# Gates and their tanh first, eight fixed expert tiles with the lists moved behind them, two shared down products in another bank, a ring of six

## What is computed

```python
x = x + tanh(g_xattn[0]) * L0_xattn(layernorm(x), ctx)   # one head, keys of 32 context tokens
x = x + tanh(g_ffn[0])   * L0_ffn(layernorm(x))          # expert choice: each of 8 experts picks 64 tokens, attends among them
x = x + tanh(g_xattn[1]) * L1_xattn(layernorm(x), ctx)   # 16 heads, mask over the context
x = x + tanh(g_ffn[1])   * L1_ffn(layernorm(x))          # mixture of experts

# L1_ffn: normed = layernorm with gamma and beta
probs = softmax(normed @ router_w.T); top_v, top_i = top_k(probs, 2); gates = softmax(top_v)
for e in range(8):                                       # swiglu: silu(gate) * up, then down; width 384
    out += comb[:, e] * swiglu(normed, gate_up_w[e], down_w[e])
out += swiglu(normed, shared_gate_up_w, shared_down_w)   # shared expert of width 128
```

## Time and profile before

| | us |
|---|---|
| median of 3 runs | 318.01 (316.6, 318.01, 321.76) |
| profiled execution | 318.32 |
| span of the profiled execution | 316.4 |
| PE, DVE, ACT, POOL busy | 273.7, 231.8, 207.7, 155.1 |

### The profile page before, as it was taken

The page is one execution under the profiler, slowest core; times in us unless marked ns, Lnnn a source line. Parts: engine busy times, 40 slices in busy tenths (PEclk is TensorE's granted clock), DMA queues, the critical chain, the costliest instruction groups (busy, mean ns, idle before and its releaser), DMA issues.

```text
span 316.4 us, 7622 instructions
## 1 busy us (share of the span) xinstructions
PE 273.7 (87%) x2454; PEld 207.2 (65%) x2454; DVE 231.8 (73%) x702; ACT 207.7 (66%) x481; POOL 155.1 (49%) x202
## 2 busy tenths in 40 slices
PE   8787996896999896999888763969899999999995
PEld 4463352455677554687666651348799999999995
DVE  4468178956987755788989967899577777777765
ACT  2765599986577678976864743534577777878530
POOL 2524289023632628625022778781027888888700
PEclk9899999999999999999999955589999999999999
DMA  7790002100349999980000111113212222201074
GB/s 210 228 362 39 1 2 85 48 3 0 134 151 190 182 189 182 190 130 0 2 1 11 35 36 43 51 51 84 57 52 79 71 77 70 68 32 37 8 233 135
DMA packets 34613, 28.13 MB, mean 89 GB/s; under 512 B 3072, under 2 KB 32389, under 8 KB 33936
## 3 DMA queue, kind: packets, MB, share of 16 engines
q1 hardware_dynamic: 32192, 23.77, 33.6%
q0 software_dynamic: 2240, 3.72, 3.6%
q10 hardware_dynamic: 144, 0.15, 0.2%
HBM read 14.15 MB, written 14.40 MB: 90 GB/s over the span
## 4 chain that ended last, share of the span: by engine, by line
PE 33%; DVE 22%; issue 14%; ACT 12%; POOL 12%; DMA 4%; SPq 1%; POOLq 0%; DVEq 0%; ACTq 0%
PE bank L1201 29%; POOL expert_rows L850 11%; ACT w_high L559 2%; ACT w_scaled L557 2%; DMA wr<-in 2%; DVE bn_raw L867 1%; DVE nm L998 1%; DVE region_k L1000 1%; DVE region_x L1160 1%; DMA region_q<-expert_rows 1%; ACT x_hat L547 1%; DVE x L899 1%; PE bank L1425 1%; DVE region_k L966 1%; ACT x_hat L671 1%
## 5 line engine op out<-in xcount | busy, mean ns | idle before, releaser
L1185 DVE TENSOR_TENSOR region_k<-region_x,region_k 128x768 f16<-128x768 f32 (+1 forms) x33 | 30.6, 927 | 21.6 <-ACT region_k L721 21.6
L1201 PE MATMUL bank<-w_scaled,w_high 128*128 128x256 f16 x252 | 42.4, 273 | 0.1
L1201 PE MATMUL bank<-w_high,region_k 128*128 (+1 forms) x380 | 37.6, 220 | 3.3 <-DVE x L1175 2.5
L850 POOL DMA_INDIRECT expert_rows<-region_k,slot_dest x22 | 27.1, 1232 | 26.4 <-DVE region_k L1172 19.1
L824 POOL DMA_INDIRECT dispatched_rows<-region_t,slot x28 | 29.0, 1036 | 16.1 <-issue 8.3
L721 ACT ACTIVATE region_k<-region_x 128x768 f16<-128x768 f32 (+1 forms) x33 | 26.8, 812 | 14.2 <-DVE region_x L1160 14.2
L1201 PE MATMUL bank<-w_scaled,w_low 128*128 128x256 f16 x126 | 34.3, 273 | 0.0
L1201 PE MATMUL bank<-w_low,region_k 128*128 (+1 forms) x190 | 33.8, 220 | 0.0
L1201 PEld LDWEIGHTS bank<-w_high,region_k 128*128 128x128 f16 x380 | 30.8, 98 | 4.5 <-issue 4.1
L1160 DVE SCALAR_TENSOR_TENSOR region_x<-bank,region_w 128x768 f32<-128x768 f32 (+1 forms) x33 | 30.4, 921 | 3.2 <-ACT region_w L726 2.1
L1201 PE MATMUL bank<-filler 128*128 128x512 f16 x94 | 27.9, 418 | 3.9 <-DVE region_k L909 2.4
(11 more groups left out here) (246 smaller groups left out, 755.5 us busy)
## 6 DMA issues: line engine op xcount, KB each, us to landing
dispatched_rows<-pad_rows SPq DMA_DIRECT2D x8, 1048.0 KB, 18.4
w_scaled<-in SPq DMA_DIRECT2D x5, 1024.0 KB, 7.8
w_scaled<-dispatched_rows SPq DMA_DIRECT2D x21, 131.0 KB, 2.2
region_q<-expert_rows SPq DMA_DIRECT2D x3, 512.0 KB, 5.1
x<-in SPq DMA_DIRECT2D x4, 256.0 KB, 3.9
region_w<-in SPq DMA_DIRECT2D x2, 512.0 KB, 7.0
out<-x SPq DMA_DIRECT2D x3, 256.0 KB, 2.8
w_scaled<-in SPq DMA_DIRECT2D x1, 704.0 KB, 4.0
```

The costliest lines, as they stand in the source:

```text
L850: pool.indirect_dma_start(ytok, bass.IndirectOffsetOnAxis(dst[:, n, h:h + 1].bitcast(U32), 0), yv[n % 4][:, h * D:(h + 1) * D], None, boun ...
L1185: dve.tensor_tensor(hsplit[:, v, k:2 * k], hid[:, v, 0:k], hsplit[:, v, 0:k], ALU.subtract).then_inc(hidden_low, 1)
L1201: return pe.matmul(o, l, r, start=start, stop=stop)
```

## The change

1. **Gates first.** The two gates are loaded at the head of ACT's queue, ahead of the constants `c32`, and the tanh stands right behind the load of the activation table. The values `v0` of the cross-attention are scaled by the first gate in the copy that takes them out of PSUM; the multiplication of `rz` on DVE is gone. `wr0` has a semaphore of its own.
2. **Eight fixed tiles.** Tile n < 8 is always the first 256 rows of expert n, at row n x 2048. SP, PE and `slot_dest` take numbers instead of loaded values for them. The other 13 (`LISTED`) come from lists half as long (`TTAB` 32 to 16). The list work leaves the shared steps 1 and 2 and stands in the steps 8, 9 and 10 (tiles 1, 2 and 3); `gates_of_all` moves from step 3 to 2. SP waits for the lists only at tile 8, PE only before tile 7.
3. **Bank 6.** The down products of shared steps 1 and 3 go to bank 6 instead of 7, and wait for the emptying of two steps before instead of one.
4. **Ring of six.** SP's loaded tiles have six places instead of four. `slot_dest` moves from two steps ahead to its tile's own step.

The core of the diff:

```diff
-ROUNDS = -(-TILES // 4)
-TTAB = 4 * ROUNDS + 8
+LISTED = TILES - E
+ROUNDS = -(-LISTED // 8)
+TTAB = 8 * ROUNDS
+RING = 6
+DOWN_IN_6 = (1, 3)
...
+        def down_bank(s):
+            return bank[6] if s in DOWN_IN_6 else bank[7]
...
-            eng.dma_start(graw[:, 0:2], gx_in...).then_inc(gates_loaded, 16)
-            eng.dma_start(graw[:, 2:4], gf_in...).then_inc(gates_loaded, 16)
-            eng.dma_start(wr0[:, 0:E], wr0_in).then_inc(gates_loaded, 16)
+            eng.dma_start(wr0[:, 0:E], wr0_in).then_inc(wr0_loaded, 16)
...
-            eng.wait_ge(tiles, 1)
-            rows = [eng.value_load(trow_i[0:1, n:n + 1], min_val=0, max_val=E * REG) for n in range(AHEAD)]
             eng.wait_ge(w_low_done, CHUNKS)
             eng.wait_ge(sent, 16 * 2 * NS)
             for n in range(TILES):
-                wait(eng, rows_turned, n - 3)
-                wait(eng, dest_ready, n - 3)
-                row = rows[n] if n < AHEAD else eng.value_load(trow_i[0:1, n:n + 1], min_val=0, max_val=E * REG)
+                wait(eng, rows_turned, n - RING + 1)
+                wait(eng, dest_ready, n - RING + 1)
+                if n == E:
+                    eng.wait_ge(tiles, 2)
+                row = n * REG if n < E else eng.value_load(trow_i[0:1, n - E:n - E + 1], min_val=0, max_val=E * REG)
...
         def _(act):
+            act.dma_start(graw[:, 0:2], gx_in...).then_inc(gates_loaded, 16)
+            act.dma_start(graw[:, 2:4], gf_in...).then_inc(gates_loaded, 16)
             act.dma_start(c32[:, :], c32_in).then_inc(c32_loaded, 16)
             nc.scalar.preload_act_table(ACT.Exp)
+            act.wait_ge(gates_loaded, 32)
+            act.activation(tg[:, :], graw[:, :], ACT.Tanh).then_inc(tanh_done, 1)
...
-                    if b == 0:
-                        act.wait_ge(gates_loaded, 48)
-                        act.activation(tg[:, :], graw[:, :], ACT.Tanh).then_inc(tanh_done, 1)
...
-            after_hidden = {0: top2_apart, 1: tiles_placed, 2: windows_packed, 3: gates_of_all}
+            after_hidden = {0: top2_apart, 2: gates_of_all, STEP_OF[1]: tiles_numbered, STEP_OF[2]: tiles_placed, STEP_OF[3]: windows_packed}
...
                 pe.wait_ge(hidden_low, s + 1)
-                wait(pe, rows_ready, s)
+                if s == DOWN_IN_6[0]:
+                    pe.wait_ge(tiles, 1)
+                wait(pe, rows_ready, s - 1 if s <= DOWN_IN_6[-1] + 1 else s)
...
                 if late:
-                    pe.wait_ge(tiles, 2)
-                    load_window(0)
-                    e = experts()
-                    load_window(1)
+                    pe.wait_ge(rows_ready, DOWN_IN_6[-1] + 1)
                     turn(0)
                     down(s - 1, None)
```

More of the change, by code:

```diff
@@ L429, in build @@
         padded = sem("padded")
-        rows_loaded = [sem(f"rows_loaded{r}") for r in range(4)]
+        rows_loaded = [sem(f"rows_loaded{r}") for r in range(RING)]
         dest_ready = sem("dest_ready")
@@ L1074, in tiles_counted, with tiles_numbered @@
                 dve.wait_ge(counts_made, 1)
-                link(dve.tensor_copy(cnt[:, :], bank[6][:, 0:E]))
-                link(dve.tensor_scalar(cnti[:, :], cnt[:, :], float(TP - 1), None, ALU.add))
+                dve.tensor_copy(cnt[:, :], bank[6][:, 0:E]).then_inc(tiles, 1)
+            def tiles_numbered():
+                dve.wait_ge(tiles, 1)
+                link(dve.tensor_scalar(cnti[:, :], cnt[:, :], -1.0, 0.0, ALU.add, ALU.max))
                 link(dve.tensor_scalar(cnti[:, :], cnti[:, :], 8, None, ALU.logical_shift_right))
@@ L1088, in tiles_placed @@
                 dve.tensor_scalar(trow_i[:, :], trow[:, :], float(E * REG), None, ALU.min).then_inc(tiles, 1)
[L1090 to L1095, removed]
+                link(dve.tensor_scalar(tw[:, :, :], te[:, :].rearrange("p (i j) -> p i j", j=8), float(E - 1), None, ALU.min))
                 link(dve.tensor_tensor(tw[:, :, :], tw[:, :, :],
@@ L1186, in _ @@
                                       ALU.subtract).then_inc(hidden_low, 1)
-                if ahead[0] == "rows" and ahead[1] < 2:
-                    slot_dest(ahead[1])
+                if s < len(STEPS) and STEPS[s][0] == "rows":
+                    slot_dest(STEPS[s][1])
                 if s == len(STEPS):
@@ L1504, in gate_up @@
                 if kind == "rows":
-                    w = [[v[:, ds(expert, 1), i * P:(i + 1) * P].rearrange("p e n -> p (e n)") for v in gu_w] for i in range(NF)]
+                    w = [[of_expert(v, expert, i * P, P) for v in gu_w] for i in range(NF)]
                     pe.wait_ge(rows_turned_out, n + 1)
@@ L1537, in down @@
                 if kind == "rows":
-                    w = [[v[:, ds(expert, 1), i * D:(i + 1) * D].rearrange("p e n -> p (e n)") for v in dn_w] for i in range(FC)]
+                    w = [[of_expert(v, expert, i * D, D) for v in dn_w] for i in range(FC)]
                 elif kind == "dense":
@@ L1572, in expert_of @@
                     return None
-                return e[n % 4] if n // 4 == n_window else before[n % 4]
+                if n < E:
+                    return n
+                return e[n % 8] if n // 8 == n_window else before[n % 8]
             n_window = 0
@@ L1587, in _ @@
                     n = STEPS[s + 1][1]
[L1588 to L1591, removed]
+                    if n == E - 1:
+                        pe.wait_ge(tiles, 3)
+                        load_window(0)
+                    elif n >= E and n % 8 == 0:
+                        before, e, n_window = e, experts(), n // 8
+                        if n // 8 < ROUNDS:
+                            load_window(n // 8)
                 if ahead[0] == "rows" and ahead[1] > 0 and not late:
```

46 lines of the change are left out of this document (24 added, 22 removed).

## The result

| | median us (runs) | ratio to before, 95% interval |
|---|---|---|
| before | 320.29 (22) | |
| changed | 317.89 (22; 315.2 to 319.15) | 0.9939 [0.9914, 0.9963] |
| changed, a second time beside other runs of before | 317.65 (12), before 319.25 (23) | 0.9987 [0.9955, 1.002] |

The ratios leave out runs more than 1.5% above the fastest of their kernel, so they stand a little above the quotient of the medians. The forecast was 314.5 in 310.8 to 317.6, 1.1% less time; the measured gain is 0.6% at the first measurement, and the time lies just above the range. At the second measurement the interval takes in 1, so the change isn't told from none there.

What follows compares the result with a forecast made beforehand. PE was taken as what the start's chain waits for, with PE and POOL's sends ending almost together. 318.32 − 3.4 (start) − 0.1 (join) = 314.8, lowered by 0.3 to the median 314.5 us; range 310.8 to 317.6.

Steps and rivals of the forecast that it cites:

- the two issues come before `c32` on ACT's queue ... I cost them at nothing: Start: issuing the two gate transfers on ACT ahead of c32 costs 0, covered by PE's fillers.
- The other three terms of the sum: Start: batch 1's normalisation earlier −1.0, early clock dip gone −1.7, rz multiplications off DVE −0.7 us.
- the 1.7 of the dip: Start: PE's half-clock stretch of 3.4 us from about 13.4 goes, worth −1.7 us, bounds 0 and −1.7.
- the likeliest case: Join: PE falls to half clock for 3.4 us after its new wait before tile 0, +1.7 us; forecast has 42%.
- the stall of 0.4: Rows steps: lists make DVE's copy of tile 1's result 1.75 late, stalling PE +0.4 us, bounds 0 and 1.75.
- the wait of 2.49: Join: PE's idle 2.49 us before 210.00, for DVE to empty bank 7, goes with lists moved and bank 6 used.
- Scatters that end earlier: Rival, join: scatters shorten by what lists cost them, the load comes up to 2.8 earlier, no dip; 310.0 us, 8%.
- POOL's chain carrying the delay: Rival, rows steps: tile 1's copy, 1.75 late, delays its two sends through to the end; 316.3 us, 10%.
- The clock staying down: Rival, join: the new wait before tile 0 starts 24 us at half clock in place of 3.4; 324.8 us, 4%.
- No dip in the rows steps: Rival, join: PE doesn't fall to half clock after its new wait before tile 0; 312.8 us, 22%.
- Nothing moves: Rival, whole kernel: PE's loads and the scatters set the join, the start's chain has another member; 318 us, 2%.
- The early dip stays: Rival, start: an idle is left at 12 us and PE's early half-clock dip remains; 316.2 us, 12%.

Runs made afterwards that it cites:

- e1: Kernel before with part 1 alone (gates first, tanh first, gate in the copy of v0): 318.46 us, ratio 1.0015.
- f1: Changed kernel with the gates loaded into one partition and spread by one PE product with a row of ones: 313.88 us, ratio 0.9877.
- g1: Kernel before with part 1 alone in the form of f1, no change at the join: 315.62 us, ratio 0.9947.
- e2: Changed kernel with part 1 undone, so the kernel before with parts 2, 3 and 4 alone: 317.98 us, ratio 0.998.
- f3: Changed kernel with the edits of f1 and f2 together: 313.3 us, ratio 0.9852.
- g2: Changed kernel run again without any edit, beside other runs of before: 317.65 us, ratio 0.9987.
- f2: Changed kernel with 24 products of ones on PE while it waits for the load of tile 0: 316.13 us, ratio 0.9958.
- f4: Changed kernel with all down products in bank 7 again (part 3 undone): 317.1 us, ratio 0.9977.
- e4: Changed kernel with down(5) ahead of the turn of tile 0 on PE instead of behind it: 317.24 us, ratio 0.999.

## Why the prediction was wrong

**The start: the step that failed is "the two issues come before `c32` on ACT's queue ... I cost them at nothing".** I priced the issue on ACT and named `c32` as what might be late, and did not price what the two transfers do to SP's first loads. The row for it stood in the trace of before: the two broadcasts of the gates, 1 KB each, took 4.4 us to land there, longer than the 256 KB of a load of x. Issued at 0.72 and 1.18 us, beside the first load of x and ahead of ctx and `wq`, they made each 2.3 to 2.5 us later. The Trainium skill (DMA: Bandwidth & Descriptors, "Issuing engines are not separate DMA queues") says that transfers from any engine end on the same 16 engines and interleave. e1 and f1 agree in so far as what ACT issues can hold up the loads of SP (x lands after 6.5 us in e1 and 3.9 in f1). The other three terms of the sum were about right for the execution that it was made against: with the broadcast gone the start gains 3.13 (f1) and 2.87 (g1) of the forecast 3.4, and the normalisation of batch 1 comes at 10.35 (f1), forecast about 10.3. But the 1.7 of the dip in it is no fixed gain. The start of before has a dip in both of its traces (before, e2) and that of f1 and g1 none in three (f1, f3, g1); a start of before without one isn't on record.

**The dips as a matter of how long PE idled.** I read that PE falls after 1.58 and 2.49 and not after 1.47 as an order by length. The changed kernel fell behind 1.33 at 55.80, where before stood at full clock behind 1.36 and the same work (PE's first row there in the changed kernel; the granted clock is 0.50 from 57 to 58 us):

```profile
55.80 0.59 PE L1204 MATMUL bank<-region_p,region_s 128*128 128x512 f16 x2 [1.33 <-DVE region_p L928]
```

With one and the same code there, g2 fell behind 1.35 (at 55.84) and f2 stood at full clock behind 1.35 (at 55.80). e1 didn't fall behind 2.15, where the changed kernel fell behind 2.13, and e2 fell where no wait exceeds 1.00. So the length of the wait doesn't decide it; what does is open. This one dip took back 1.06 us between the start and the scatters: a gain of 0.57 at 29 us had become a loss of 0.49 at the first scatter (171.93 against 171.44). f2, without it, has 141.59 us from the start to the first scatter, as before has (141.62), where the changed kernel has 142.68.

**The join was better than its sum**: −0.8 instead of −0.1. The turn of tile 0 came 1.53 nearer to the scatters (forecast 1.4). From that turn to gate_up of tile 1 the changed kernel takes 6.24, before 5.77: +0.47, forecast +0.9. The dip came behind the new wait as the likeliest case had it, at the price of 1.66 (f2; forecast 1.7), the idle 0.81 went, and 0.38 more went that the sum didn't have; 0.22 of this lies between the turn just ahead of gate_up of tile 1 and that product (0.44 before, 0.22 changed). From gate_up of tile 1 to the last send the changed kernel has 72.98 (225.83 to 298.81), before 72.74 (226.37 to 299.11): +0.24 in place of the stall of 0.4, and no idle of PE between 236 and 240. The copy of tile 1 was late as worked out (237.07), and it cost no more than that. The two profiled executions thus differ by −0.57 in the start, +1.06 for the dip at 56 us and −0.82 in the join, which makes up the 0.3 between them.

My reason for the wait of 2.49, lists and bank together, was not refuted: f4 has another piece of DVE's work in the lists' place, and the wait with it.

**The rivals.** Scatters that end earlier: out, 43.7 us from the first to the last scatter's end in both. The send at 207.11, counted there as beside a list operation, began when `tiles_placed` had ended (207.09), and the changed kernel has a send of 1.43 at 203.62 with no list operation near. POOL's chain carrying the delay: out (f2, and the +0.24). The clock staying down: out, 3.4 us. "No dip in the rows steps": out for the changed kernel, whose two traces both have it. "Nothing moves", 318, came nearest in time, for another reason than its own. "The early dip stays" came true, for a wait that I hadn't seen.

**The range** hung on a median of three runs, 2.3 us below that of 22 runs, though within the spread of the other sets' medians (317.86 to 319.25). On the baseline of the 22 the forecast's 1.1% would be 316.8, and the measured time would lie 1.1 us above it. The traces account for 0.3 us of gain; what the medians show beyond it goes in part with less time at half clock (g2), which the sum didn't foresee. So far the nearness of the time to the range is luck.

## What to carry to other kernels

A transfer is not priced by its issue or its bytes alone: look up how long its like took from issue to landing, and what lands behind it; a few values that all partitions need, as the gates here, were better loaded once and spread by a product. For PE's waits of 1.3 to 2.2 us here, the length didn't tell whether the clock falls behind them, so count such a dip in the range and not as a sure term, and fill the wait if it can be filled (f2). An experiment that takes one cause away has to leave no other work in its place (f4). Where executions differ by 2%, three runs don't fix the baseline of a 1% forecast.

## What the runs showed of the hardware

Beside two broadcasts of 1 KB each, written as 8 bytes to each of 128 partitions, the transfer engines moved 137 GB/s in place of 360 in the microsecond shown (349 in f1), at a lower busy share, and every first load of SP landed more than 2 us later. The stretches at half clock were 3.4, 6.8, 10.2, 20.5 or 23.9 us long in the twelve profiles (those cut off by the end of the span aside), and the same kernel had another set of them in another execution (the changed kernel four, and a fifth at 165 us in g2). The record of the granted clock isn't complete: in e4 products took twice their time from 8.15 us on at a recorded 1.00.
